# SyncE's order of transfers in a gated slot attention kernel: the fp8 store ahead of the s and value weights, w ahead of e, q weights behind e

## The reference, cut to what matters

```
z = cumlogsumexp(s);  p = exp(s - z);  g = exp(z_prev - z)
hk = hk * g + k (x) p         ok = q . hk        # keys into slots
w  = softmax(ok)
hv = hv * g + p (x) v         o  = w . hv        # values out of slots
o  = o * rsqrt(mean(o^2) + eps) * gnorm * silu(x Wg)
x  = x + o Wo
x  = x + (silu(n Wgate8 * sg) * (n Wup8 * su)) Wdown8 * sd      # n: layer norm of x
```

## Time and profile before

| | |
|---|---|
| median of three runs | 1340.43 us |
| the profiled execution, its own time | 1341.52 us |
| its span, first to last instruction | 1339.8 us |
| TensorE busy (PE) | 1323.1 us, 99% of the span |
| VectorE busy | 1057.4 us, 79% |
| ScalarE busy | 428.2 us, 32% |
| GpSimd busy | 137.3 us, 10% |
| DMA: share of the 16 engines, queue of SyncE | 48.2% |
| mean granted TensorE clock | 0.999 of full |

### The profile page before, as it was taken

The page is one execution under the profiler, slowest core; times in us unless marked ns, Lnnn a source line. Parts: engine busy times, 40 slices in busy tenths (PEclk is TensorE's granted clock), DMA queues, the critical chain, the costliest instruction groups (busy, mean ns, idle before and its releaser), DMA issues.

```text
span 1339.8 us, 24318 instructions
## 1 busy us (share of the span) xinstructions
PE 1323.1 (99%) x9303; PEld 1099.2 (82%) x9303; DVE 1057.4 (79%) x1684; ACT 428.2 (32%) x1287; POOL 137.3 (10%) x106
## 2 busy tenths in 40 slices
PE   8999999999999999999999999999999999999998
PEld 7887888788878888888888888878888888888887
DVE  8888888888878888888888888888778776755454
ACT  5433323332323233323323332333233333232221
POOL 3001101110111012001200210011010010000000
PEclk9999999999999999999999999999999999999999
DMA  6157555655665566556555655566442564120000
GB/s 189 40 116 176 113 117 121 163 122 117 137 147 119 111 148 136 120 117 155 133 128 115 162 127 134 119 151 136 85 107 44 155 165 87 47 49 31 0 32 32
DMA packets 532241, 150.88 MB, mean 113 GB/s; under 512 B 385185, under 2 KB 523297, under 8 KB 532129
## 3 DMA queue, kind: packets, MB, share of 16 engines
q1 hardware_dynamic: 532128, 149.37, 48.2%
HBM read 88.95 MB, written 60.36 MB: 111 GB/s over the span
## 4 chain that ended last, share of the span: by engine, by line
PE 72%; DVE 10%; SPq 7%; DMA 7%; issue 3%; ACT 1%; DVEq 0%; ACTq 0%
PE bank L493 14%; PE bank L118 13%; PE bank L495 12%; PE bank L494 12%; PE bank L1789 6%; SPq L372 4%; PE bank L735 3%; SPq L336 2%; PE bank L718 2%; DMA fp_weights<-q 2%; PE bank L583 2%; DMA e_tokens<-k_tok_then_wT 2%; PE bank L563 2%; DMA k_tok_then_wT<-w_slots 1%; PE bank L723 1%
## 5 line engine op out<-in xcount | busy, mean ns | idle before, releaser
L493 PE MATMUL bank<-wvg_hi,xT_hi 128*128 128x512 f32 x512 | 206.7, 404 | 0.7
L495 PE MATMUL bank<-wvg_hi,xT_lo 128*128 128x512 f32 x512 | 199.9, 390 | 0.0
L494 PE MATMUL bank<-wvg_lo,xT_hi 128*128 128x512 f32 x512 | 199.8, 390 | 0.0
L828 ACT ACTIVATE a_and_v<-bank 128x256 f32<-128x256 f32 x128 | 49.0, 383 | 324.7 <-PE bank L495 324.6
L493 PEld LDWEIGHTS bank<-wvg_hi,xT_hi 128*128 128x128 f32 x512 | 96.2, 188 | 25.0 <-issue 3.6
L495 PEld LDWEIGHTS bank<-wvg_hi,xT_lo 128*128 128x128 f32 x512 | 96.1, 188 | 20.6
L494 PEld LDWEIGHTS bank<-wvg_lo,xT_hi 128*128 128x128 f32 x512 | 96.3, 188 | 17.8
L1170 DVE RECIPROCAL cT<-cT 128x512 f32<-128x512 f32 x32 | 107.0, 3342 | 0.0
L1115 POOL TENSOR_TENSOR rstd<-ssq,neg_half 128x8 f32<-128x8 f32 x32 | 52.4, 1637 | 506.0 <-DVE ssq L1218 506.0
L493 PE MATMUL bank<-wo_hi,oT_hi 128*128 128x512 f32 x256 | 99.8, 390 | 0.0
L495 PE MATMUL bank<-wo_hi,oT_lo 128*128 128x512 f32 x256 | 99.6, 389 | 0.0
(11 more groups left out here) (180 smaller groups left out, 3045.8 us busy)
## 6 DMA issues: line engine op xcount, KB each, us to landing
o_transposed<-o SPq DMA_DIRECT2D x27, 512.0 KB, 3.5
oT_lo<-o_transposed SPq DMA_DIRECT2D x108, 128.0 KB, 3.1
fp_weights<-q SPq DMA_DIRECT2D x28, 318.0 KB, 3.3
e_tokens<-k_tok_then_wT SPq DMA_DIRECT2D x31, 256.0 KB, 2.3
e_tok<-e_tokens SPq DMA_DIRECT2D x124, 64.0 KB, 2.3
c_tokens<-cT SPq DMA_DIRECT2D x31, 256.0 KB, 2.4
cT<-c_tokens SPq DMA_DIRECT2D x124, 64.0 KB, 2.3
w_slots<-p SPq DMA_DIRECT2D x27, 256.0 KB, 2.4
```

Of the source, the lines that this page charges most:

```text
L493: pe.matmul(dst, w_hi, m_hi, start=(k == 0), stop=False)
L494: pe.matmul(dst, w_hi, m_lo, start=False, stop=False)
L495: last = pe.matmul(dst, w_lo, m_hi, start=False, stop=(k == n - 1))
L828: return act.activation(dst, src, ACT.Copy)
```

## The change

Three edits in SyncE's list and one added wait. No transfer is added, removed or resized, and no other engine's instructions change.

1. At i = 1 `store_q8(u)` is issued ahead of the loads of the next pair's s weights and value and gate weights, where it stood behind them.
2. In units 2 to 28 `load_w(u)` is issued ahead of `load_e(u+1)`, where it stood behind it. `load_w` has a wait of its own now for the store of e (`s_est`), which `load_e` made before it.
3. At i = 2 the load of the q weights is issued directly behind `load_e`, where it stood behind `store_o` and `store_k`.

```diff
         def load_w(u):
 
+            sp.wait_ge(s_est, 16 * (u + 1))
             sp.wait_ge(s_wst, 16 * (far_before(u) + 1))
             load_blocks(wT[:, :], w_dram, s_wld)
...
             store_e(u + 1)
             if u in W_FAR:
                 store_w(u)
+                load_w(u)
             load_e(u + 1)
-            if u in W_FAR:
-                load_w(u)
+            if i == 2:
+                load_skq(pair, 2)
             if u - 1 <= FAR:
                 store_o(u - 1)
             store_k(u + 1)
-            if i == 2:
-                load_skq(pair, 2)
             if i == 3:
                 load_o(pair, 0)
...
             store_c(u + 1)
             load_k(u + 1)
             load_c(u + 1)
+            store_q8(u)
             if i == 1:
                 load_skq(pair, 0)
                 load_vg(pair)
-            store_q8(u)
```

## The result

| | before | after |
|---|---|---|
| median, same chip | 1341.70 us (4 runs) | 1333.35 us (4 runs, 1332.97 to 1333.52) |
| ratio | | 0.9932, 95% interval 0.9916 to 0.9947 |
| profiled execution, its own time | 1341.52 us | 1333.25 us |
| its span | 1339.8 us | 1331.5 us |

The change makes the kernel 8.4 us faster by the medians (7.1 to 11.3 by the interval of the ratio) and 8.3 us by the two profiled executions; 1334.0 was forecast. The median before is 1341.70 and not 1340.43, because a fourth run of 1344.89 came with the comparison.

The account below looks back on a forecast made before the run. TensorE, busy 99% of the span, was taken as the bound, so only its idle time could go. Idle 7.0 plus clock 1.66 less 1.0 remaining made 7.7 us off 1341.52: 1333.9, stated as 1334.0, range 1332.0 to 1338.0.

Parts of the forecast that it names:

- The sum: Whole kernel: 7.0 us of idle plus 1.66 of clock, less 1.0 of remaining stall, a net gain of 7.7 us.
- left over: Stall remaining at L718: 0.5 us in unit 6 and 0.5 for slow w stores, 1.0 in all, bounds 0 and 5.2.
- the clock term: Unit 10, L718 to L572: the lower clock behind the stall cost 1.66 us, counted once, to go with the stall.
- Its price: The s weights, issued behind the fp8 store, come 0.45 to 2.3 us later; 1.0 was taken.
- edit 2's margin: Unit 10: w's loads land at 379.9 against 381.31 wanted, 1.4 us of margin, 0.4 with the s weights late.
- Room 4.5 us, used 1.9 to 2.1: cost nothing: Unit 9, end of the o loads to the c store: delayed loads of e, o and k fit without cost.
- Rival C: Slower: e behind w delays the o loads, c store and k loads; L572 waits in all 27 units; 1346 us, chance 0.06.
- What is late next: L572 of the unit behind unit 10: 3.54 us sooner, k loads in with 1.5 us of room, 0.5 with s late.
- B: Rival: s weights, 2.3 us late, stall all seven i = 2 units, 5.2 us remaining; 1338.1 us, chance 0.16.
- D: Rival: the w or e store lands as late as before for other reasons; gain below 2 us, 1340, chance 0.09.
- E: Rival: GpSimd's earlier low part of the k weights clashes ahead of w's turning, some 2 us; 1335.9, chance 0.08.
- up to 0.9 us either way: Unit 9's tail: a clash between GpSimd and VectorE that moves away could shift it by up to 0.9 us.

Follow-up runs that it names:

- run 3: Kernel before with only the q weights loaded ahead of the o and k stores at i = 2: 1343.57 us, ratio 1.0020.
- run 5: Kernel before with only the fp8 store moved between the s weights and the value weights, e still ahead of w: 1337.69 us, ratio 0.9950.
- run 2: Kernel before with only w loaded ahead of e, and the added wait for the store of e: 1333.70 us, ratio 0.9942.
- run 1: Kernel before with only the fp8 store moved ahead of the s and value weights: 1337.81 us, ratio 0.9972.
- run 7: Changed kernel with four 512-byte DRAM copies issued behind the loads of e in each unit: 1356.01 us, ratio 1.0099.
- run 8: Changed kernel with ten 512-byte DRAM copies issued behind the loads of e in each unit: 1472.34 us, ratio 1.0963.
- run 6: Changed kernel with VectorE making the low parts of the value weights ahead of turning o at i = 3: 1332.75 us, ratio 0.9918.

## Why the prediction was right, and where it was not

**The sum.** 7.0 of idle and 1.66 of clock less 1.0 left over made 7.7; the profiled executions differ by 8.3. The idle was right: no wait of L718. Unit 10's stretch at 0.50 went too. What the sum didn't have: nothing was left over at L718, where 1.0 was taken; 0.6 us of lateness at L718 that the view of waits doesn't list went as well; and the head took 0.7. These nearly cancel, which is luck. So is the clock term as far as it goes into the difference of the two executions: what unit 10 gave back, the head lost.

**The clock has to be read from many executions.** I counted one fall, the one in the trace of before; six waits of the same total in run 3 had none. The seven executions of before whose mean clock was 1.0 took 1339.4 us on average, the 14 at 0.997 took 1344.3; the five of after at 1.0 took 1333.8. At equal clock the change is worth 5.6 us. The mean clock is 0.9980 over 45 executions of before and 0.9991 over 10 of after, which makes some 1.5 us more. The rest of the 8.4 isn't accounted for; these executions are from more than one chip and few.

**Edit 1: mechanism right, worth nearly nothing once edit 2 is in.** The store early, the fp8 loads directly behind the last value load, the e store right behind VectorE: all as written. The fp8 loads were to come 3.9 us sooner; from unit 9's L718 (now at 346.56) they stand 17.7 us off, against 22.2 before, so 4.6. Its price was mis-sized a little: from its issue to its landing the s load takes 4.3 us on average, 0.9 more than before, and the slot adds 0.53: 1.4 where I took 1.0. The Trainium skill (DMA: Bandwidth & Descriptors, section Queues, rings and completion order) has each DMA engine consume a queue's descriptors in ring order; the estimate by it was 1.2 us. The trace agrees in size. Run 5 shows that it isn't all: the s load took 5.0 to 5.2 us in three units as the first of the list.

**Edit 2: the step that carried the result was under-read.** I had the two edits as partners, each taking about 2 us out of w's way. Run 2 shows edit 2 enough by itself (the loads of w go out as soon as both stores have landed, and no longer 1.2 to 1.3 us later behind the issues of e), and run 1 shows that edit 1 by itself puts part of what it frees into late s weights. The step that failed is the attribution: I worked out edit 2's margin only with edit 1 in it, 1.4 us less the delay of s, and never the margin of each alone.

**The cover of the delayed loads.** "Room 4.5 us, used 1.9 to 2.1: cost nothing" holds by its outcome, with L572 at 0.5 us. But I read the room in unit 9, a quiet one. Rival C's point of decision at i = 2, 1.6 us on top of what the change uses, is what run 7 found. The paragraph "What is late next" had L572's room at 1.5 us, or 0.5 with s late. The trace after has less: the k loads land 0.26 us ahead of L572 in unit 10 and 0.05 in unit 6, and in unit 2 TensorE waits 0.25 us.

**Edit 3 at nothing:** no gain, as written; whether it costs something is open (run 3).

**Rivals.** B: all seven units wait for s, as its first half says, but by 1.4 us and not 2.3, and with w first it reaches no L718. D: every transfer moved as the change says. E: not seen in the seven units, where w is turned 6.0 us behind L682 plus what `ws_hi` waited, in each. A clash of that kind moved away elsewhere, at i = 1. There the load of the output weights goes later with w first, and GpSimd's low part of them with it. Before, in unit 9, the operation stood beside VectorE's fp8 step; after, it is 1.4 us further behind L718 (5.09 for 3.71):

```profile
352.72 1.78 POOL L1076 TENSOR_TENSOR wo_lo<-stage,wo_hi 128x512 fp32r<-128x512 f32 x1 [6.22 <-ACT wo_hi L828]
```
```profile
351.65 1.28 POOL L1076 TENSOR_TENSOR wo_lo<-stage,wo_hi 128x512 fp32r<-128x512 f32 x1 [7.60 <-ACT wo_hi L828]
```

L1311, another step of that rounding, in unit 9 before and after:

```profile
353.39 1.80 DVE L1311 TENSOR_TENSOR q<-q,q8t 128x636 f32<-128x636 f32 x1
```
```profile
350.94 0.82 DVE L1311 TENSOR_TENSOR q<-q,q8t 128x636 f32<-128x636 f32 x1
```

The turning of c ends 7.0 us behind L718 in unit 9 after and 8.0 before, and so the tail of unit 9 does run 1 us sooner: the "up to 0.9 us either way" of edit 1 went to the good side, though by edit 2 (run 1, edit 1 alone, has 8.0 there still, run 2 has 7.0). The Trainium skill (GPSIMD Engine Reference, Key points) says that GpSimd shares its SBUF interfaces with VectorE and contends with its instructions of two SBUF inputs; L1311 is one, and the trace agrees, with 1.80 us against 0.82.

## What to carry to other kernels

Where two edits attack one wait, work out each one's margin alone as well as both together: the one that takes issues out from directly behind the late store was worth all of it, the one further up moved its gain into another late load. Read the room for pushed transfers in every kind of unit and not in a quiet one alone (before the change 4.5 us in unit 9 and 1.9 in unit 10; after it 2.5 and 1.6). When only microseconds of stalls are at stake, count the falls of the clock over several executions, since one trace shows too few, and compare a stretch between two fixed lines as well as the whole time, since here the head alone differs by up to 4 us.

## What the runs showed of the hardware

- Behind waits of TensorE the granted clock can fall to 0.50 (1.2 GHz) and need not: it did behind 1.88 us in unit 10 before and 1.83 us in the head after, and didn't behind 2.28 us in the head before nor behind the six of up to 1.5 us in run 3. With many waits the falls add up: a mean of 0.971 with 24 waits of up to 4.5 us at one line (run 8), against 0.998 with four waits of up to 1.8 us after.
- One load that was first in SyncE's order took 5.0 to 5.2 us to land in units 2, 6 and 10, and 3.1 to 3.5 in the other four (run 5).
- A late operand can cost TensorE 0.38 us per unit (14.71 against 14.33) without a row in the view of waits; comparing the distance between two fixed lines over units found it (run 6).
- An issue of a copy of 512 bytes in DRAM held SyncE 0.6 to 0.9 us (runs 7 and 8), while one of four loads of w took 0.48 (1.92 for four).
